# Message sums in four 128x32 tiles, edge products of a whole group in one burst, nodes two turns sooner

## The chip, the cores and the metric

One core of a Trainium2 chip runs the whole layer. The metric is the device time of one execution in microseconds (us); the time of the kernel before is the median of three runs.

## The reference, cut to what matters

One graph layer on 8192 nodes of 256 features and 131072 edges of 64 features, all float32. The edges come sorted by their destination `dst`.

```python
ea  = edge_attr @ w_e + b_e                       # 131072 x 256
msg = relu(x[src] + ea)
agg = segment_sum(msg, dst, num_segments=8192)
h_local = bn(relu((x + agg) @ w1 + b1) @ w2 + b2 + x)
# attention in 256 blocks of 32 nodes, 4 heads of 64
h_attn  = bn(softmax(q @ k.T / 8) @ v @ out_w.T + out_b + x)
out = h_local + h_attn
out = bn(out + relu(out @ m_w1 + m_b1) @ m_w2 + m_b2)
result = layernorm(x + out)
```

## The kernel before, in words

**Groups.** The edges are cut into 128 groups of 1024, a group into 8 tiles of 128 edges, two tiles to a "pair" q (512 pairs in all, four to a group). One group falls on some 64 neighbouring nodes.

**One pair's way.** GpSimd (POOL) gathers the rows x[src] of its two tiles with two indirect DMAs (line 368) into one of 8 buffers `xg`; it may overwrite the buffer when VectorE (DVE) has used it. DVE adds the bias and writes the sum into one of four banks `EA` of PSUM (`seed`, line 592). For that it waits for the gather and for the message of the pair four before (`s_msg`), which has the same bank. TensorE (PE) adds the edge products onto the bank (`products`, line 774; one call does two pairs with 4 matmuls of 64 rows, two side by side, in 8 instructions since a float32 matmul is two). ScalarE (ACT) takes the relu to `msg` (`message`, line 393).

**One group's sum.** DVE makes a one-hot matrix per tile (`make_onehot`, line 601): which of the W nodes of a window an edge belongs to. The group's tiles are split into SUB = 2 halves of TS = 4 tiles, each with its own window of W = 64 nodes that starts at the half's least `dst`. `sum_group` (line 789) multiplies one-hot and messages into bank `G`, half 0 to partitions 0 to 63 and half 1 to 64 to 127: 8 matmuls, 16 instructions. ACT copies `G` to `agg` (line 398), PE transposes it back into `G` (`transpose_agg`, line 798), and DVE adds the windows onto the columns of `aggT` (`add_agg`, line 624). The windows' places are data: `add_agg` begins with one `value_load` per window (line 608), which DVE's sequencer does, and only then waits and adds. Windows may overlap, so each add waits for the one before it. `sum_group(n)` waits with `s_added` until the windows of group n-1 are added, since both use `G`.

**Attention and nodes.** 16 slabs J of 512 nodes pass q, k, scores (`sc`), `soft`max, v and `av`; 22 blocks b of nodes pass w1, B (the products with out_w and w2), m1, m2, T (transposes) and the norm (`log`, `y`). 12 blocks have 512 nodes, 6 have 256, the last 4 have 128. PE works into one bank for attention and one for nodes, and each stage waits for the engine that empties the bank.

**Order.** Every engine runs its own list, in order, over 264 turns. The tables `HEADS`, `NODES`, `FIRST_256`, `NODES_128` and `SUMS` say in which turn a stage comes. Within a turn PE does products, the transposes of an earlier sum, a group's sum, attention, nodes; ACT does messages, copy, attention, nodes; DVE does seeds, `add_agg`, one-hot, attention, nodes. The queue of SP issues the loads of edge features (`load_ea`), xT, x rows (`xn`) and the stores, also turn by turn. Two turns make one group. In the steady part 16 turns (8 groups) serve one slab and one block.

**What is where before.** `products(t)` comes in every turn t, `seed(2t+2)` and `seed(2t+3)` in turn t, `sum_group(n)` in turn 2n+3 (2n+2 for the last four), its transposes and adds one turn later. Stage w1 of block b < 12 comes in turn 16b+21 and waits for the adds of all groups that reach its nodes and one more, and for the residual rows (line 688, in stage T) of the block before.

Of the kernel before, what the change touches and what calls it, by code (L numbers as in the profile page):

```python
# [31 lines left out]
BN_SCALE = 1.0 / (1.0 + 1e-5) ** 0.5  # L32
LN_EPS = 1e-5
PER = N // NG
SUB = 2
TS = TG // SUB
W = P // SUB
FULL = 512
NJ = N // FULL
RB = FULL // P  # L40
# [13 lines left out]
def heads_base(J):  # L54
# [7 lines left out]
         "T": (14, 15), "log": (15, 16), "y": (16, 17), "xn": (8, 9), "out": (17, 18)}  # L62
NODES_256 = {"w1": (0,), "B": (1,), "z": (2,), "m1": (2, 3), "m2": (4,), "T": (5,), "log": (6,),
             "y": (7,), "xn": (2,), "out": (8,)}
FIRST_256 = {12: 213, 13: 219, 14: 225, 15: 231, 16: 237, 17: 245}
NODES_128 = {
# [8 lines left out]
}  # L75
LASTB = 21


SUMS = {(2 * n + 3 if n < NG - 4 else 2 * n + 2): n for n in range(NG)}
TURNS = 264  # L80
CHUNKS = {"w1": CC, "B": CC, "m1": 2 * CC, "m2": CC}

# [20 lines left out]
def nodes_in(turn, stages):  # L103
    found = []
    for b in range(len(BLOCKS)):
        if b < 12:
            plan, base = NODES, 16 * b + 21
        elif b < 18:
            plan, base = NODES_256, FIRST_256[b]
        else:  # L110
            plan, base = NODES_128[b], 0
        found += [(b, s, n) for s in stages for n, at in enumerate(plan[s]) if base + at == turn]
    return found
# [25 lines left out]
def gnn_layer(nc, t, out):  # L139

    k = Kept()
    k.t, k.out = t, out
    k.sum_dram = nc.dram_tensor("sum_dram", (N, C), fp32, kind="Internal").ap()
    k.oT_dram = nc.dram_tensor("oT_dram", (IT, P, CC, NB), fp32, kind="Internal").ap()
    with ExitStack() as ctx:
        def sb(name, shape, dt=fp32):
            return ctx.enter_context(nc.sbuf_tensor(name, shape, dt))

        k.bank = [ctx.enter_context(nc.psum_tensor(f"bank{n}", [P, 512], fp32)) for n in range(8)]
        k.EA, k.G = k.bank[0:4], k.bank[4]  # L150
# [12 lines left out]
        k.bad = sb("bad", [P, 1])  # L163
        k.srcs = sb("srcs", [P, NG * TG], i32)
        k.rel = sb("rel", [P, NG, TG])
        k.we = sb("we", [P, C])
        k.iwT, k.owT = sb("iwT", [P, CC, 3 * C]), sb("owT", [P, CC, C])
        k.w1, k.w2 = sb("w1", [P, CC, C]), sb("w2", [P, CC, C])
        k.m1, k.m2 = sb("m1", [P, CC, 2 * C]), sb("m2", [P, 4, C])

        k.xg = sb("xg", [P, NX, 2 * C])
        k.ea = sb("ea", [P, NEA, 4 * P])
        k.msg = sb("msg", [P, NM, 2 * C])
        k.onehot = sb("onehot", [P, 2, TG, W])
        k.agg = sb("agg", [P, C])
        k.be_rows = k.agg

        k.xT = sb("xT", [P, NXT, CC, FULL])
        k.qT = sb("qT", [P, CC, FULL])
        k.kbd = sb("kbd", [P, CC, FULL // W, 2, W])  # L180
        k.vn = k.qT[:, :, :].rearrange("p c (a n) -> p (c a) n", n=C)
        k.dif, k.probT = sb("dif", [P, RB, H, NPG]), sb("probT", [P, 2, 2 * H, P])
        k.ex = k.prob = k.dif
        k.mx, k.sm, k.rs = sb("mx", [P, 2 * H]), sb("sm", [P, 2 * H]), sb("rs", [P, 2 * H])
        k.oT = sb("oT", [P, NOT, CC, FULL])

        k.h1, k.o = sb("h1", [P, CC, FULL]), sb("o", [P, CC, FULL])
        k.z, k.h2 = sb("z", [P, CC, FULL]), sb("h2", [P, 4, FULL])
        k.xn = sb("xn", [P, 2, 2, C])
        k.y = k.xn  # L190

        k.dst_g = k.h2[:, 0:2, :].rearrange("p c n -> p (c n)").bitcast(i32)
        k.dst_p = k.oT[:, 0, :, :].rearrange("p c (g t) -> p (c g) t", t=TG).bitcast(i32)
        k.gammas = k.xn[:, :, :, :].rearrange("p a b c -> p (a b) c")[:, 0:3, :]
        k.stats, k.mv = sb("stats", [P, 2, 2, 6]), sb("mv", [P, 2, 2, 2])
        k.logv, k.root = sb("logv", [P, 2, 2]), sb("root", [P, 2, 2])
        k.rstd, k.fix = sb("rstd", [P, 2]), sb("fix", [P, 2])
        program(nc, k)


def program(nc, k):
# [3 lines left out]
    with ExitStack() as ctx:  # L205
        def sem(name):
            return ctx.enter_context(nc.semaphore(name))
# [15 lines left out]
        s_seed, s_prod, s_msg = (sem(n) for n in ("s_x_seeded", "s_ea_product", "s_msg_made"))  # L223
        s_seg, s_agg, s_aggT, s_added = (sem(n) for n in (
            "s_group_summed", "s_agg_copied", "s_agg_transposed", "s_agg_added"))
        s_oh, s_half = sem("s_onehot_made"), sem("s_first_half_added")
        s_pre = [sem(f"s_agg_preloaded_{n}") for n in range(2)]

        s_xT = [sem(f"s_xT_loaded_{n}") for n in range(NXT)]
# [148 lines left out]
        def _(act):  # L378
# [21 lines left out]
            def attention(J, stage, n):  # L400
# [7 lines left out]
                if stage == "k":  # L408
# [3 lines left out]
                    for h in range(2):  # L412
                        of = slice(h * DH, (h + 1) * DH)
                        ins = nc.scalar.activation(
                            k.kbd[of, n, :, h, :], X[of, :].rearrange("p (r n) -> p r n", n=W),
                            ACT.Identity, bias=vecT[of, V_INB + 2 + n:V_INB + 3 + n])
                    ins.then_inc(s_qkc, 1)
                if stage == "soft":
# [45 lines left out]
                                         scale=-0.5).then_inc(s_root, 1)  # L464

            for turn in range(TURNS):
                for q in (2 * turn, 2 * turn + 1):
                    if q < NP:
                        message(q)
                if turn in SUMS:  # L470
                    copy_agg(SUMS[turn])
# [9 lines left out]
        def _(dve):  # L481
# [43 lines left out]
            for sub in range(SUB):  # L525
# [5 lines left out]
            step_of(ins)  # L531
            nc.vector.tensor_copy(k.base_i[:, :, :].rearrange("p s n -> p (s n)"),
                                  X[:, 0:SUB * P])
            step_of(nc.vector.tensor_reduce(k.bad[:, :], X[:, SUB * P:(SUB + 1) * P], AX.X,
                                            ALU.max))
            settle()
            nc.vector.tensor_copy(k.bad_i[:, :], k.bad[:, :]).then_inc(s_spread, 1)

# [68 lines left out]
            def add_agg(n):  # L607
# [11 lines left out]
                sums = G[:, 0:C].rearrange("p (c n) -> p c n", n=P)  # L619
                for sub in range(SUB):  # L620
                    if sub:
                        dve.wait_ge(s_half, n + 1)
                    window = aggT[:, :, bass.ds(at[sub], W)]
                    nc.vector.tensor_tensor(window, sums[:, :, sub * W:(sub + 1) * W], window,  # L624
                                            ALU.add).then_inc(s_added if sub else s_half, 1)

            def attention(J, stage, n):
                quarter = [slice(m * NPG, (m + 1) * NPG) for m in range(P // NPG)]
                scores = k.XA[:, :].rearrange("p (a n) -> p a n", n=W)
                dif = k.dif[:, 2 * n:2 * n + 2, :, :].rearrange("p r h n -> p (r h) n")  # L630
                if stage == "sc":
                    dve.wait_ge(s_sc, 2 * J + n + 1)
# [80 lines left out]
                                                      k.rstd[:, m:m + 1], ALU.subtract, ALU.mult)  # L713
                    ins.then_inc(s_y, 1)

            seed(0)
            seed(1)
            make_onehot(0)
            for turn in range(TURNS):
                for q in (2 * turn + 2, 2 * turn + 3):  # L720
                    if q < NP:
                        seed(q)
                if turn == 0:
                    nc.vector.memset(k.kbd[0:DH, :, :, 1, :], 0.0)
                    nc.vector.memset(k.kbd[DH:P, :, :, 0, :], 0.0).then_inc(s_kbd, 1)
                if turn == 1:
                    step_of(nc.vector.memset(k.probT[:, :, :, :], 0.0))
                    settle()
                if turn - 1 in SUMS:
                    add_agg(SUMS[turn - 1])  # L730
                if turn % 2 == 1 and 1 <= turn // 2 < NG:
                    make_onehot(turn // 2)
                weights(turn)
                for J, stage, n in heads_in(turn, ("sc", "soft")):
                    attention(J, stage, n)
# [7 lines left out]
        def _(pe):  # L743
# [12 lines left out]
                                           start=n == 0, stop=n == 3, skip_group_check=True)  # L756
            ins.then_inc(s_set, 1)
            pe.wait_ge(s_base, 1)
            for n, row in enumerate((k.lohi[:, 2, 0:1], k.lohi[:, 2, 1:2], k.lohi[:, 0, 0:1])):
                ins = nc.tensor.transpose(X[:, n * P:(n + 1) * P], row.to_broadcast([P, P]),  # L760
                                          ident[:, :])
            ins.then_inc(s_baseT, 1)
            pe.wait_ge(s_we, 16)

# [56 lines left out]
            def attention(J, stage, n):  # L821
# [13 lines left out]
                if stage == "sc":  # L835
# [4 lines left out]
                    for r in range(2):  # L840
                        for c in range(CC):
                            for m in range(2):
                                two = 4 * n + 2 * r + m
                                col = r * C + c * P
                                ins = nc.tensor.matmul(  # L845
                                    XA[m * W:(m + 1) * W, col:col + P],
                                    k.qT[:, c, two * W:(two + 1) * W],
                                    k.kbd[:, c, two, :, :].rearrange("p h n -> p (h n)"),
                                    start=True, stop=True)
                    ins.then_inc(s_sc, 1)  # L850
# [96 lines left out]
                    ins.then_inc(s_t, 1)  # L947

            for turn in range(TURNS):
                if turn < ND:  # L950
                    products(turn)
                if turn - 1 in SUMS:
                    transpose_agg(SUMS[turn - 1])
                if turn in SUMS:
# [315 lines left out]
```

## Time and profile before

| | |
|---|---|
| median of 3 runs | 1321.83 us (1321.43 to 1322.18) |
| profiled execution | 1321.81 us, its span 1321.8 us |
| PE busy | 1242.6 us (94%) |
| DVE, ACT, POOL busy | 819.9, 552.5, 970.7 us |
| granted TensorE clock | 0.98 of full speed on average |

Busy time is the union of an engine's instructions. Matmuls overlap, so PE's stretches are best read from one start to the next. DVE's sequencer reads window places beside its engine's work, and such time is not counted as busy. POOL's busy time leaves out 0.3 us between two gathers.

### The profile page before, as it was taken

To read this page: it belongs to the slowest core of one execution; us is meant where nothing else is said; L and a number is where in the kernel's file an instruction comes from. 1 tells how busy PE (TensorE), PEld (TensorE's weight loads), DVE (VectorE), ACT (ScalarE), POOL (GpSimd) and SP (SyncE) were. 2 spreads that over 40 slices of the span, in tenths; PEclk is the share of its full clock that TensorE was granted. 3 is DMA by queue.
4 is the path that set the end of the run, shared out by engine and by line. 5 is a ranking of instruction groups with operands and counts; after the bars stand their busy time and mean duration, and the time that the engine had idled before them with its cause. 6 is when DMAs were issued, how large, how long until landed. Compare 5 with 4: busy or idle time off the path is not lost.

```text
span 1321.8 us, 21000 instructions
## 1 busy us (share of the span) xinstructions
PE 1242.6 (94%) x7307; PEld 729.6 (55%) x7307; DVE 819.9 (62%) x1831; ACT 552.5 (42%) x1077; POOL 970.7 (73%) x1032
## 2 busy tenths in 40 slices
PE   5797999999999999999999999999999999999997
PEld 3454555555555555555555545555455556767676
DVE  4757456657475575746667475575746657548554
ACT  1343434444344434444443444443444434444443
POOL 7777777777777777777777777777777777777760
PEclk7897999999999999999999999999999999999999
DMA  9454645555555555555555555555555555545540
GB/s 325 137 177 144 180 136 160 170 173 177 158 155 168 170 169 162 177 160 162 170 162 177 152 156 167 170 170 155 162 176 164 168 158 155 184 146 151 178 140 18
DMA packets 113259, 216.02 MB, mean 163 GB/s; under 512 B 21505, under 2 KB 62721, under 8 KB 113153
## 3 DMA queue, kind: packets, MB, share of 16 engines
q0 software_dynamic: 49152, 134.28, 35.1%
q1 hardware_dynamic: 62560, 77.09, 18.1%
q10 hardware_dynamic: 1440, 3.29, 0.7%
q8 instruction: 59, 0.97, 0.3%
q14 instruction: 48, 0.39, 0.1%
HBM read 197.80 MB, written 16.78 MB: 162 GB/s over the span
## 4 chain that ended last, share of the span: by engine, by line
PE 55%; POOL 19%; DVE 11%; issue 9%; DMA 4%; DVEq 1%; ACT 1%
PE bank L746 28%; POOL xg L368 19%; PE bank L774 12%; PE bank L789 11%; DMA xg<-in_x_dram,srcs 4%; DVE bank L592 3%; PE bank L798 2%; DVE mx L635 2%; DVE dif L640 1%; PE bank L871 1%; PE bank L845 1%; DVEq L608 1%; DVE o L667 1%; DVE aggT L624 1%; DVE probT L656 1%
## 5 line engine op out<-in xcount | busy, mean ns | idle before, releaser
L368 POOL DMA_INDIRECT xg<-in_x_dram,srcs x1024 | 969.8, 947 | 313.5 <-issue 297.0
L393 ACT ACTIVATE msg<-bank 128x512 f32<-128x512 f32 x512 | 277.7, 594 | 392.7 <-PE bank L774 392.2
L592 DVE TENSOR_TENSOR bank<-xg,bank 128x512 f32<-128x512 f32 x512 | 337.3, 690 | 157.8 <-DMA xg<-in_x_dram,srcs 132.4
L774 PE MATMUL bank<-we,ea 64*128 64x256 f32 x2048 | 297.8, 410 | 55.5 <-DVE bank L592 55.5
L774 PEld LDWEIGHTS bank<-we,ea 64*128 64x128 f32 x2048 | 182.0, 190 | 205.4 <-issue 146.8
L789 PE MATMUL bank<-msg,onehot 128*64 128x256 f32 x2048 | 254.7, 392 | 4.0 <-DVE aggT L624 4.0
L789 PEld LDWEIGHTS bank<-msg,onehot 128*64 128x64 f32 x2048 | 139.8, 139 | 103.7 <-issue 47.8
L624 DVE TENSOR_TENSOR aggT<-bank,aggT 128x128 f32 x256 | 74.7, 292 | 187.4 <-PE bank L798 142.7
L746 PE MATMUL bank<-xT,iwT 128*128 128x512 f32 x256 | 125.8, 614 | 6.6 <-DMA xT<-in_xT_dram 6.6
L746 PE MATMUL bank<-o,m 128*128 128x512 f32 (+2 forms) x352 | 122.8, 483 | 0.0
L746 PE MATMUL bank<-h,m 128*128 128x512 f32 (+2 forms) x352 | 116.8, 479 | 1.0 <-ACT h L453 1.0
L398 ACT COPY agg<-bank 128x256 f32<-128x256 f32 x128 | 47.6, 372 | 113.1 <-PE bank L789 113.1
L601 DVE TENSOR_TENSOR onehot<-bank,rel 128x512 f32<-128x512 f32 x128 | 87.6, 684 | 0.2
L746 PEld LDWEIGHTS bank<-h,m 128*128 128x128 f32 x352 | 60.1, 191 | 40.4 <-issue 36.9
L746 PEld LDWEIGHTS bank<-o,m 128*128 128x128 f32 x352 | 59.6, 191 | 31.2 <-issue 28.2
L676 DVE TENSOR_TENSOR z<-bank,z 128x512 f32<-128x512 f32 (+2 forms) x44 | 23.1, 543 | 86.3 <-PE bank L746 86.1
L453 ACT ACTIVATE h<-bank,mb 128x512 f32<-128x512 f32 (+2 forms) x88 | 47.6, 569 | 68.2 <-PE bank L746 68.2
L746 PEld LDWEIGHTS bank<-xT,iwT 128*128 128x128 f32 x256 | 44.1, 192 | 51.4 <-issue 51.0
L746 PE MATMUL bank<-oT,owT 128*128 128x512 f32 (+2 forms) x176 | 64.6, 491 | 0.6 <-ACT h L439 0.6
L746 PE MATMUL bank<-iwT,xT 128*128 128x256 f32 x256 | 64.3, 396 | 0.0
L746 PE MATMUL bank<-h,w 128*128 128x512 f32 (+2 forms) x176 | 62.2, 477 | 0.0
L746 PE MATMUL bank<-aggT,w 128*128 128x512 f32 (+2 forms) x176 | 61.3, 480 | 0.8 <-DVE xn L688 0.8
(88 smaller groups left out, 927.0 us busy)
## 6 DMA issues: line engine op xcount, KB each, us to landing
ea<-in_ea_dram SPq DMA_DIRECT2D x128, 256.0 KB
xg<-in_x_dram,srcs POOLq DMA_INDIRECT x1024
xT<-in_xT_dram SPq DMA_DIRECT2D x32, 256.0 KB, 3.9
aggT<-in_xT_dram SPq DMA_DIRECT2D x32, 256.0 KB, 5.0
oT_dram<-oT SPq DMA_DIRECT2D x32, 256.0 KB
xn<-in_x_dram SPq DMA_DIRECT2D x32, 256.0 KB, 5.1
out_dram<-xn SPq DMA_DIRECT2D x30, 256.0 KB, 2.8
m<-in_m_dram ACTq DMA_DIRECT2D x2, 512.0 KB, 17.9
```

The costliest lines, as they stand in the source:

```text
L368: pool.indirect_dma_start(xg[:, q % NX, n * C:(n + 1) * C], None, t["x"], bass.IndirectOffsetOnAxis(k.srcs[:, at:at + 1], 0)).then_inc(s_x ...
L393: nc.scalar.activation(msg[:, q % NM, :], EA[q % 4][:, :], ACT.Relu).then_inc(s_msg, 1)
L398: nc.scalar.copy(k.agg[:, :], G[:, 0:C]).then_inc(s_agg, 1)
L453: ins = nc.scalar.activation(k.h2[:, c, at], bank(b, "m1")[:, of], ACT.Relu, bias=k.mb1[:, c:c + 1])
L592: nc.vector.tensor_tensor(EA[q % 4][:, :].rearrange("p (a c) -> p a c", a=2), xg[:, q % NX, :].rearrange("p (a c) -> p a c", a=2), KB[:, 0 ...
L601: nc.vector.tensor_tensor(onehot[:, n % 2, :, :], KB[:, C:C + W].unsqueeze(1).to_broadcast([P, TG, W]), k.rel[:, n, :].unsqueeze(2).to_bro ...
L624: nc.vector.tensor_tensor(window, sums[:, :, sub * W:(sub + 1) * W], window, ALU.add).then_inc(s_added if sub else s_half, 1)
L635: ins = nc.vector.tensor_reduce(k.mx[g, :], scores[g, :, own], AX.X, ALU.max)
L746: ins = nc.tensor.matmul(to, stationary(c), moving(c), start=start and c == 0, stop=stop and c == blocks - 1, skip_group_check=skip)
L774: ins = nc.tensor.matmul(EA[(2 * d + pair) % 4][:, two * C:(two + 1) * C], ea[rows, n % NEA, at:at + P], k.we[rows, :], start=False, stop= ...
L789: ins = nc.tensor.matmul(G[sub * W:(sub + 1) * W, 0:C], onehot[:, n % 2, at, :], msg[:, q % NM, two * C:(two + 1) * C], start=tile == 0, s ...
L798: ins = nc.tensor.transpose(G[:, c * P:(c + 1) * P], k.agg[:, c * P:(c + 1) * P], ident[:, :])
```

## The change

SUB becomes 4: four sub-groups of two tiles, each with a window of 32 nodes and 32 partitions of `G`; the sum still takes 8 matmuls, of 32 instead of 64 columns of the one-hot. `add_agg` reads four places and makes four adds, each after the one before. The one-hot has 256 instead of 512 elements in a partition. Products of a whole group (two calls) come in turn 2n, its sum in turn 2n+1, transposes and adds in turn 2n+2. The seeds of group n+1 come in turn 2n: two, then the adds of group n-1, then two. The one-hot of group n+1 comes in turn 2n+1. All stages of nodes come two turns sooner (the last block one). Attention stays in its turns; it had used W = 64 for its own layout and now uses GW = 64.

```diff
-SUB = 2
+SUB = 4
 TS = TG // SUB
 W = P // SUB
+GW = 2 * NPG
-FIRST_256 = {12: 213, 13: 219, 14: 225, 15: 231, 16: 237, 17: 245}
+FIRST_256 = {12: 211, 13: 217, 14: 223, 15: 229, 16: 235, 17: 243}
...
-SUMS = {(2 * n + 3 if n < NG - 4 else 2 * n + 2): n for n in range(NG)}
+SUMS = {2 * n + 1: n for n in range(NG)}
...
-            plan, base = NODES, 16 * b + 21
+            plan, base = NODES, 16 * b + 19
...
 # ScalarE, each turn
-                for q in (2 * turn, 2 * turn + 1):
-                    if q < NP:
+                if turn % 2 == 0 and turn // 2 < NG:
+                    for q in range(2 * turn, 2 * turn + PG):
                         message(q)
...
 # add_agg
                 for sub in range(SUB):
                     if sub:
-                        dve.wait_ge(s_half, n + 1)
+                        dve.wait_ge(s_part, (SUB - 1) * n + sub)
                     window = aggT[:, :, bass.ds(at[sub], W)]
                     nc.vector.tensor_tensor(window, sums[:, :, sub * W:(sub + 1) * W], window,
-                                            ALU.add).then_inc(s_added if sub else s_half, 1)
+                                            ALU.add
+                                            ).then_inc(s_added if sub == SUB - 1 else s_part, 1)
...
 # VectorE, each turn
-                for q in (2 * turn + 2, 2 * turn + 3):
-                    if q < NP:
-                        seed(q)
+                ahead = turn // 2 + 1
+                if turn % 2 == 0 and ahead < NG:
+                    seed(PG * ahead)
+                    seed(PG * ahead + 1)
+                if turn - 1 in SUMS:
+                    add_agg(SUMS[turn - 1])
+                if turn % 2 == 0 and ahead < NG:
+                    seed(PG * ahead + 2)
+                    seed(PG * ahead + 3)
...
-                if turn - 1 in SUMS:
-                    add_agg(SUMS[turn - 1])
-                if turn % 2 == 1 and 1 <= turn // 2 < NG:
-                    make_onehot(turn // 2)
+                if turn % 2 == 1 and ahead < NG:
+                    make_onehot(ahead)
...
 # TensorE: setup spreads four window starts instead of two (and the check value into G)
-            for n, row in enumerate((k.lohi[:, 2, 0:1], k.lohi[:, 2, 1:2], k.lohi[:, 0, 0:1])):
+            for n, row in enumerate(k.lohi[:, 2, sub:sub + 1] for sub in range(SUB)):
...
 # TensorE, each turn
-                if turn < ND:
+                if turn % 2 == 0 and turn < ND:
                     products(turn)
+                    products(turn + 1)
```

## Rows read from the trace of the kernel before

**Rows 1.** The page's chain that ended last, shares of the span by engine.

```profile
PE 55%; POOL 19%; DVE 11%; issue 9%; DMA 4%; DVEq 1%; ACT 1%
```

**Rows 2.** Line 368, the gathers: duration ns min/median/max, first and last start.

```profile
L368 POOL DMA_INDIRECT xg<-in_x_dram,srcs x1024: 940/946/1397, 3.4 to 1284.1; - x171
```

**Rows 3.** Waits, whole span: who waited for whom, us in total, times, longest.

```profile
POOL xg L368 <- DVE bank L592: 14.8, 48, 0.4
...
PE bank L789 <- DVE aggT L624: 4.0, 7, 1.0
```

**Rows 4.** Timeline of PE: start, us, line, out<-in, count [idle before <-releaser].

```profile
425.74 1.14 PE L774 MATMUL bank<-we,ea 64*128 64x256 f32 x8
426.80 1.95 PE L789 MATMUL bank<-msg,onehot 128*64 128x256 f32 x16
428.58 1.04 PE L871 MATMUL bank<-probT,qT 128*64 128x128 f32 x16
429.55 1.13 PE L774 MATMUL bank<-we,ea 64*128 64x256 f32 x8
430.62 0.44 PE L798 MATMUL bank<-ident,agg 128*128 128x128 f32 x2
430.89 3.60 PE L746 MATMUL bank<-h,m 128*128 128x512 f32 x8
...
446.30 1.88 PE L746 MATMUL bank<-aggT,w 128*128 128x512 f32 x4
```

**Rows 5.** Timeline of PE, the one regular wait, in two periods of 16 turns.

```profile
400.52 1.14 PE L774 MATMUL bank<-we,ea 64*128 64x256 f32 x8 [2.39 <-DVE bank L592]
...
478.46 2.04 PE L774 MATMUL bank<-we,ea 64*128 64x256 f32 x8 [2.39 <-DVE bank L592]
```

**Rows 6.** Stretch after the second: us, busy by engine, granted clock, DMA.

```profile
480.00:482.00 2.00, 2.00 (x9) 1.39 (x6) 1.93 (x5) 1.08 (x2) 1.39 (x3) 0.51 1.12 391
```

**Rows 7.** Timeline early: products, their messages, a seed that waits for these.

```profile
30.60 1.14 PE L774 MATMUL bank<-we,ea 64*128 64x256 f32 x8
...
31.78 1.09 ACT L393 ACTIVATE msg<-bank 128x512 f32<-128x512 f32 x2 [0.39 <-PE bank L774]
...
32.48 1.29 DVE L592 TENSOR_TENSOR bank<-xg,bank 128x512 f32<-128x512 f32 x2 [1.65 <-ACT msg L393]
```

**Rows 8.** Line 608, the reads of window places, by DVE's sequencer.

```profile
L608 DVEq TENSOR_LOAD <-base_i x256: 297/305/954, 36.4 to 1302.0; - x128
```

**Rows 9.** Timeline of DVE: a seed, and the adds after two reads.

```profile
616.28 0.70 DVE L592 TENSOR_TENSOR bank<-xg,bank 128x512 f32<-128x512 f32 x1 [0.96 <-DMA xg<-in_x_dram,srcs]
617.72 0.72 DVE L624 TENSOR_TENSOR aggT<-bank,aggT 128x128 f32 x2 [0.74 <-issue]
```

**Rows 10.** Groups by line and shape: busy us, mean ns | idle before.

```profile
L624 DVE TENSOR_TENSOR aggT<-bank,aggT 128x128 f32 x256 | 74.7, 292 | 187.4 <-PE bank L798 142.7 <-issue 25.6 <-DVE aggT L624 1.0
...
L499 DVE COPY bank<-iota 128x64 f32<-128x64 f32 x1 | 0.2, 228 | 1.8 <-POOL even L357 1.8
```

**Rows 11.** Timeline of DVE: scores (two lines) and softmax, up to the next seeds.

```profile
698.98 1.71 DVE L635 TENSOR_REDUCE mx<-bank 32x8 f32<-32x256 f32 x4
700.72 1.72 DVE L640 TENSOR_TENSOR dif<-bank,mx 32x256 f32<-32x256 f32 x4
...
704.94 0.41 DVE L647 TENSOR_REDUCE sm<-dif 128x8 f32<-128x256 f32 x1
...
707.90 1.29 DVE L592 TENSOR_TENSOR bank<-xg,bank 128x512 f32<-128x512 f32 x2
```

**Rows 12.** Timeline of PE: products of turns 46 and 254, the last sum.

```profile
256.12 1.13 PE L774 MATMUL bank<-we,ea 64*128 64x256 f32 x8
...
1289.90 1.14 PE L774 MATMUL bank<-we,ea 64*128 64x256 f32 x8
...
1298.11 1.95 PE L789 MATMUL bank<-msg,onehot 128*64 128x256 f32 x16
```

**Rows 13.** Chain of waits, in order of time: a gather, from issue to landing.

```profile
731.06 2.74 DMA xg<-in_x_dram,srcs
```

More of the change, by code:

```diff
@@ L179, in gnn_layer @@
         k.qT = sb("qT", [P, CC, FULL])
-        k.kbd = sb("kbd", [P, CC, FULL // W, 2, W])
+        k.kbd = sb("kbd", [P, CC, FULL // GW, 2, GW])
         k.vn = k.qT[:, :, :].rearrange("p c (a n) -> p (c a) n", n=C)
@@ L225, in program @@
             "s_group_summed", "s_agg_copied", "s_agg_transposed", "s_agg_added"))
-        s_oh, s_half = sem("s_onehot_made"), sem("s_first_half_added")
+        s_oh, s_part = sem("s_onehot_made"), sem("s_window_added")
         s_pre = [sem(f"s_agg_preloaded_{n}") for n in range(2)]
@@ L414, in attention @@
                         ins = nc.scalar.activation(
-                            k.kbd[of, n, :, h, :], X[of, :].rearrange("p (r n) -> p r n", n=W),
+                            k.kbd[of, n, :, h, :], X[of, :].rearrange("p (r n) -> p r n", n=GW),
                             ACT.Identity, bias=vecT[of, V_INB + 2 + n:V_INB + 3 + n])
@@ L533, in _ @@
                                   X[:, 0:SUB * P])
-            step_of(nc.vector.tensor_reduce(k.bad[:, :], X[:, SUB * P:(SUB + 1) * P], AX.X,
-                                            ALU.max))
+            step_of(nc.vector.tensor_reduce(k.bad[:, :], G[:, 0:P], AX.X, ALU.max))
             settle()
@@ L621, in add_agg @@
                     if sub:
-                        dve.wait_ge(s_half, n + 1)
+                        dve.wait_ge(s_part, (SUB - 1) * n + sub)
                     window = aggT[:, :, bass.ds(at[sub], W)]
                     nc.vector.tensor_tensor(window, sums[:, :, sub * W:(sub + 1) * W], window,
-                                            ALU.add).then_inc(s_added if sub else s_half, 1)
+                                            ALU.add
+                                            ).then_inc(s_added if sub == SUB - 1 else s_part, 1)
             def attention(J, stage, n):
                 quarter = [slice(m * NPG, (m + 1) * NPG) for m in range(P // NPG)]
-                scores = k.XA[:, :].rearrange("p (a n) -> p a n", n=W)
+                scores = k.XA[:, :].rearrange("p (a n) -> p a n", n=GW)
                 dif = k.dif[:, 2 * n:2 * n + 2, :, :].rearrange("p r h n -> p (r h) n")
@@ L714, in node @@
                     ins.then_inc(s_y, 1)
-            seed(0)
-            seed(1)
+            for q in range(PG):
+                seed(q)
             make_onehot(0)
             for turn in range(TURNS):
-                for q in (2 * turn + 2, 2 * turn + 3):
-                    if q < NP:
-                        seed(q)
+                ahead = turn // 2 + 1
[7 more added lines that the diff above has]
+                    seed(PG * ahead + 3)
                 if turn == 0:
@@ L758, in _ @@
             pe.wait_ge(s_base, 1)
-            for n, row in enumerate((k.lohi[:, 2, 0:1], k.lohi[:, 2, 1:2], k.lohi[:, 0, 0:1])):
+            for n, row in enumerate(k.lohi[:, 2, sub:sub + 1] for sub in range(SUB)):
                 ins = nc.tensor.transpose(X[:, n * P:(n + 1) * P], row.to_broadcast([P, P]),
                                           ident[:, :])
+            ins = nc.tensor.transpose(G[:, 0:P], k.lohi[:, 0, 0:1].to_broadcast([P, P]),
+                                      ident[:, :])
             ins.then_inc(s_baseT, 1)
@@ L845, in attention @@
                                 ins = nc.tensor.matmul(
-                                    XA[m * W:(m + 1) * W, col:col + P],
-                                    k.qT[:, c, two * W:(two + 1) * W],
+                                    XA[m * GW:(m + 1) * GW, col:col + P],
+                                    k.qT[:, c, two * GW:(two + 1) * GW],
                                     k.kbd[:, c, two, :, :].rearrange("p h n -> p (h n)"),
```

16 rows, old and new, of the table NODES_128 are left out of this document.

## The prediction

> **What bounds the kernel now.** I read the chain first, then the waits, then the timelines. The chain gives PE 55% and POOL 19% [rows 1], so two engines compete. The gathers are a metronome: 1024 starts from 3.4 to 1284.1 us [rows 2], one per 1.252 us, and what POOL waited for buffers is 0.3 us each time [rows 3], no more than its gap between any two gathers. Eight groups (64 gathers) so cost 80.1 us whatever else is done, and the kernel ends 37 us after the last gather. PE is nearly as full: in its timeline each burst starts where the one before stops [rows 4], and its one regular wait of 2.39 us returns after 478.46 - 400.52 = 77.9 us, which is 16 turns or 8 groups [rows 5]. With that pace it catches up with the gathers by 2 us per 8 groups. Sums never really wait for the adds: 4.0 us in all [rows 3]. A change thus gains only in the 37 us at the end, but loses as soon as some loop needs over 10.0 us per group.
>
> **The change, part by part.** Times of PE are from start to start [rows 4]: products 1.06, transposes 0.27, sum 1.78, av 0.97, m2 or B 3.6, w1, q, k, v or one use of m1 1.8. Scores I take like av.
>
> *Sum.* Still 16 instructions. No row shows 32 columns; below, four side by side need half the time of two, 0.9 us; above, no gain, 1.78 (side by side not at all: 3.6). I take 0.95, since 64 columns show what side by side does. PE gains 0.85 per group, and two products in one burst 1.9 instead of 2.1: about 1.05 in all, 8.4 per 8 groups. Alone this moves nothing, as the gathers don't get faster.
>
> *Adds.* Two reads of window places become four, two adds four. From a seed's start to the add behind it pass 617.72 - 616.28 = 1.44 us with two reads [rows 9], though the data were there ("issue"); a read begins with a load of 0.305 [rows 8] and takes 0.6 with its checks. Four: 2.65 us. An add of 128 columns takes 0.292 and starts 0.43 after the one before (0.72 for two [rows 9, 10]); with 64 columns I take 0.225 like the copy of that size [rows 10], bounds 0.15 and 0.29, so 0.36 apart and 1.3 for four. The one-hot halves, 0.3 us less on DVE.
>
> *Order.* This decides. Before, a turn's seeds wait for messages of the turn before, so DVE can run ahead and reads the places early. Now the first seeds of group n+1 wait for messages of group n, whose products come in the same turn; the reads stand behind these seeds, the adds of n-1 behind the reads, and the sum of n, one turn later, behind the adds. From the start of a burst: message 1.18 later, seed 0.70 after that [rows 7], sum 1.88; second seed issued 0.45 later; reads 2.65; adds 1.3; a semaphore 0.1. So a sum starts at least 6.4 us after its burst, where PE has only 1.9 + 0.27 + the even turn's attention and nodes (E) to do. Then 0.95 for the sum and the odd turn's work (O). A pair of turns takes the larger of 7.35 + O and 3.1 + E + O. Queued behind the sum are O and the next products; behind the adds on DVE two seeds, the scores, softmax and residual adds.
>
> *Steady part.* With the new tables, by turn modulo 16:
> - 14, 15: E m2, O av: 8.4.
> - 0, 1: m2; av, T. T waits for the z add behind the seeds, 8.45: 9.05.
> - 2, 3: T; w1. w1 waits for the residual rows of T, behind four seeds on DVE (7.7 + 0.7): 10.25, though PE works 5.5.
> - 4, 5: q, w1; q: 9.2.
> - 6, 7: k, B; k: 10.35.
> - 8 to 13: DVE bound. Scores 3.45, softmax 2.95 [rows 11]. The first burst is late by k's and z's copies on ACT: seeds and adds end at 8.8; scores, o 0.75, one-hot 0.35, softmax: 16.3; seeds, adds, seeds (reads hidden) 4.05, scores, one-hot, softmax: 27.1; seeds and adds: sum of turn 13 at 29.9; with v and m1 34.5.
>
> Sum 81.75 per 8 groups, against 77.9 that PE and DVE need before and 80.1 of the gathers: the new loop is slower than both.
>
> *Last part.* Turns 210 to 253, 22 pairs in which blocks come denser (256 nodes per 6 turns). By the same rule: 10.25, 12.2, 12.75, then 28.0 for turns 216 to 219 (w1 behind the residual rows behind the scores, then m1 behind y, scores and o on DVE), 12.75, 10.25, 10.5, 10.95, 11.05, 12.2, 25.4 for turns 232 to 235 likewise, 12.2, 11.9, 8.4, 9.2, 10.5, 11.95, 9.3, 10.6, 9.3: 249.7.
>
> *End.* From the products of turn 254 to the last sum 7.4 (w1 of block 20 now waits for adds of the same turn). From the last sum to the end: 1321.8 - 1298.1 = 23.7 before [rows 12]; block 20 is one turn further ahead and the sum shorter, 2 less, while four reads and adds cost 1.7 and the norm of block 20 stands ahead of block 21's rows, 1.2: 24.65.
>
> *The rest.* Nodes two turns sooner keep their distance from the sums, so nothing by itself; their loads and stores pass SP's queue in front of loads of edge features, 0.3 to 0.6 us each, two turns ahead of need: 0, and if that cover went, a load late by as much per block, below 20 us. Setup: one transpose more, four subtractions for two, a larger cast, 0.9 us ahead of seeds that wait for their first gathers: 0, at worst 0.9. POOL's waits: four buffers free in one burst, needed two groups later; with the loop late, POOL waits for it.
>
> **The sum.** Turn 46 starts at 256.1 before [rows 12]. Up to there the start's costs are alike (first gathers, loads of weights), so I keep it, within -4 and +8. Ten times 81.75 to turn 206, 17.45 to turn 210, 249.7 to turn 254, 7.4 and 24.65: 256.1 + 817.5 + 17.45 + 249.7 + 7.4 + 24.65 = 1372.8, say **1372 us**, 50 slower (3.8%). The profiled execution (1321.81) and the median (1321.83) agree, so nothing is added. An error of 0.2 us in the 6.4 makes some 15 us over 128 groups. If the middle stays below 80.1, the gathers set it, and turn 210 starts with the first four tiles of group 105: 3.4 + 105 x 10.015 + 3 x 1.252 + 2.74 + 0.7 = 1062 [rows 2, 13], which ends at 1344. Own range 1340 to 1402.
>
> *The clock.* After the wait of 2.39 us the products took 2.04 instead of 1.14 [rows 5], and the granted clock was 0.51 in 480 to 482, the lower level [rows 6]; after 400.52 it stayed high. So such a wait can cost 1.7 us of PE. The new order makes waits of 3.7 (turn 2) and 4.0 (turn 10) in each 16 turns, before work on the loop: 0 to 2 x 1.7 per 8 groups, up to 30 us. I take none, but the upper end reaches there. The Trainium skill (TensorE: Matmul & The Clock Gate, "HAM oscillation") says that idle gaps in a loop throttle the clock again, and speaks against the change; by it the sum would be about 1400.
>
> **Rivals.**
> - *The loop stays below the gathers, so the change is faster.* For it: PE's work falls to 67 of 80 us. It decides if the sum starts less than about 5.5 us after its burst, so if reads overlap the seeds or messages come sooner. Then the last data land at 1284.1 + 2.74 = 1286.85 [rows 2, 13]; seed 0.7, products 1.15, messages 1.1: 1289.8; with PE's work in between the last sum starts at 1290.4, not 1298.1, and the end is 1315. Against: rows 9, where reads cost time with a seed running.
> - *It cancels*: the middle on the gathers, and in the last part lag only as large as before: 1319 to 1324.
> - *32-column tiles don't run four at a time*, so that the change doesn't do what it says: sums 0.85 longer in nearly every pair, 6 per 8 groups and 19 at the end, so about 1450. Against: two at a time do so now.
>
> **Chances.** Forecast 0.72, of which the gathers bound the middle in about a third; faster 0.14; cancelled 0.07; no four-fold tiles 0.07. Range 1322 to 1402: it leaves out the faster case and what lies above. What a measurement can tell from no change is 0.2%, 2.6 us: faster 0.14, same 0.07, slower 0.79.
>
> **What would show it.** Right: PE waits before line 789 grow from 4 us to some 2 us per group, with DVE's adds as releaser; the sum's 16 instructions take about 1 us; adds start 2.6 us after the second seed; gathers wait for seeds in the second half, or the time from the last gather to the end grows far beyond 37 us. Wrong: PE's waits stand before line 774 with the gathers behind them, gathers keep 1.252 us, and the end comes within 32 us of the last.

## The result, and the profile after

The changed kernel takes 1462.4 us (median of 4 runs, 1455.8 to 1462.7) against 1322.0 of the kernel before: ratio 1.105, 95% interval 1.1037 to 1.1064. The forecast was 1372 us with a range of 1322 to 1402: the direction was right, the size was not; the loss is 140 us, where 50 were forecast.

The page's chain of the changed kernel, by engine and then by line. Beside [rows 1] POOL has left it, and DVE's sequencer (DVEq) has grown from 1% to 15%, nearly all of it the reads of window places (L608).

```profile
PE 42%; DVE 25%; DVEq 15%; issue 10%; ACT 7%; DMA 1%; SPq 0%
PE bank L751 23%; DVEq L608 13%; PE bank L796 8%; PE bank L781 7%; DVE aggT L624 7%; DVE bank L592 6%; ACT msg L394 4%; DVE dif L641 3%; DVE mx L636 3%; PE bank L878 2%; DVEq L624 1%; DVE probT L657 1%; ACT z L448 1%; ACT kbd L415 1%; DMA xT<-in_xT_dram 1%
```

Its waits, as us in total, times, longest. The sums (L796) waited 4.0 us for the adds [rows 3], now 198.8; the gathers waited 14.8 us for the seeds, now 145.1. The second row shown is DVE standing ahead of its adds for what the profile calls issue: the reads.

```profile
DVE bank L592 <- ACT msg L394: 284.5, 86, 6.8
DVE aggT L624 <- issue: 208.4, 119, 2.4
...
PE bank L796 <- DVE aggT L624: 198.8, 106, 6.5
POOL xg L369 <- DVE bank L592: 145.1, 74, 8.3
```

One regular pair of turns (142, 143) in PE's timeline. Products come as one burst, and the sum has the short form (16 instructions of 32 columns take 1.07 us, those of 64 columns 1.95 before; from its start to the next instruction 1.00 and 1.78 [rows 4]), but it starts 6.48 us after the burst's start, with PE waiting for the last 0.68:

```profile
794.51 2.00 PE L781 MATMUL bank<-we,ea 64*128 64x256 f32 x16
796.44 0.44 PE L805 MATMUL bank<-ident,agg 128*128 128x128 f32 x2
796.72 3.60 PE L751 MATMUL bank<-h,m 128*128 128x512 f32 x8
800.99 1.07 PE L796 MATMUL bank<-msg,onehot 128*32 128x256 f32 x16 [0.68 <-DVE aggT L624]
```

The same loop on DVE in these turns: two seeds at +1.88, 1.86 us of issue (the first of the 2.4 us of reads run beside the second seed), four adds from +5.03, and only then the other two seeds.

```profile
796.39 1.29 DVE L592 TENSOR_TENSOR bank<-xg,bank 128x512 f32<-128x512 f32 x2 [5.14 <-ACT msg L394]
799.54 1.30 DVE L624 TENSOR_TENSOR aggT<-bank,aggT 128x64 f32 x4 [1.86 <-issue]
800.76 1.28 DVE L592 TENSOR_TENSOR bank<-xg,bank 128x512 f32<-128x512 f32 x2
```

The instructions of line 608: duration ns min/median/max, first and last start. A read is a load and, to check its bounds, a register operation and an assertion; with the gaps that makes 0.61 us, and the four stand one after the other.

```profile
L608 DVEq TENSOR_LOAD <-base_i x512: 296/304/668, 31.4 to 1441.4; - x171
L608 DVEq FUSED_REGOPS  x512: 183/183/206, 32.0 to 1441.7; - x171
L608 DVEq SEQ_ASSERT  x512: 23/23/35, 32.2 to 1442.3; - x171
```

Twice per 16 turns the wait is longer, and there the clock falls. PE's timeline at turn 66 and, below it, the window behind (columns: length of the window, busy time and count of PE, PEld, DVE, ACT, POOL, granted clock, DMA share, GB/s):

```profile
473.50 0.60 PE L952 MATMUL bank<-ident,z 128*128 128x128 f32 x4
477.82 1.93 PE L796 MATMUL bank<-msg,onehot 128*32 128x256 f32 x16 [3.73 <-DVE aggT L624]
479.69 3.55 PE L751 MATMUL bank<-aggT,w 128*128 128x512 f32 x4
```

```profile
478.00:483.00 5.00, 5.00 (x20) 1.65 (x15) 3.90 (x13) 0.87 (x3) 3.78 (x5) 0.51 0.37 107
```

Behind the wait of 3.73 us the granted clock is 0.51, the lower level of 1.2 GHz; the sum takes 1.93 instead of 1.07 and w1 3.55 instead of 1.88. Over the whole span the granted clock stands below full for 267 us, before for 64.

By the starts of the products in PE's timeline, in the profiled executions (the spans are 1321.8 and 1461.0):

| stretch | before | forecast | after |
|---|---|---|---|
| start to turn 46 | 256.1 | 256.1 | 282.1 |
| turns 46 to 205, per 8 groups | 79.0 | 81.75 | 85.5 |
| turns 206 to 209 | 17.6 | 17.45 | 18.0 |
| turns 210 to 253 | 225.9 | 249.7 | 276.2 |
| turn 254 to the end | 31.9 | 32.05 | 29.9 |

### The profile page after: what moved, and what is told of

Same layout as the page of the kernel before. It is cut to its first block, busy times and chain, and to the rows that moved or that the text cites. A ratio compares the mean times of both kernels' runs of the same rounds, so it can differ in the third digit from the quotient of the medians.

```text
span 1461.0 us, 22286 instructions
## 1 busy us (share of the span) xinstructions
PE 1195.7 (82%) x7309; PEld 692.5 (47%) x7309; DVE 821.4 (56%) x2089; ACT 541.6 (37%) x1077; POOL 970.4 (66%) x1032
## 3 DMA queue, kind: packets, MB, share of 16 engines
q0 software_dynamic: 49152, 134.28, 31.9%
## 4 chain that ended last, share of the span: by engine, by line
PE 42%; DVE 25%; DVEq 15%; issue 10%; ACT 7%; DMA 1%; SPq 0%
PE bank L751 23%; DVEq L608 13%; PE bank L796 8%; PE bank L781 7%; DVE aggT L624 7%; DVE bank L592 6%; ACT msg L394 4%; DVE dif L641 3%; DVE mx L636 3%; PE bank L878 2%; DVEq L624 1%; DVE probT L657 1%; ACT z L448 1%; ACT kbd L415 1%; DMA xT<-in_xT_dram 1%
## 5 line engine op out<-in xcount | busy, mean ns | idle before, releaser
L796 PE MATMUL bank<-msg,onehot 128*32 128x256 f32 x2048 | 160.4, 436 | 198.8 <-DVE aggT L624 198.8
L394 ACT ACTIVATE msg<-bank 128x512 f32<-128x512 f32 x512 | 264.4, 602 | 99.1 <-PE bank L781 97.5
L781 PE MATMUL bank<-we,ea 64*128 64x256 f32 x2048 | 266.5, 401 | 6.5 <-DVE bank L592 6.5
L624 DVE TENSOR_TENSOR aggT<-bank,aggT 128x64 f32 x512 | 115.1, 225 | 264.3 <-issue 208.4
L781 PEld LDWEIGHTS bank<-we,ea 64*128 64x128 f32 x2048 | 194.6, 194 | 106.2 <-issue 83.2
L796 PEld LDWEIGHTS bank<-msg,onehot 128*32 128x32 f32 x2048 | 67.1, 119 | 302.8 <-issue 289.2
L751 PE MATMUL bank<-o,m 128*128 128x512 f32 (+2 forms) x352 | 144.1, 550 | 10.2 <-DVE o L668 10.2
L751 PE MATMUL bank<-aggT,w 128*128 128x512 f32 (+2 forms) x176 | 88.2, 650 | 15.7 <-DVE xn L689 10.4
L751 PEld LDWEIGHTS bank<-aggT,w 128*128 128x128 f32 x176 | 40.7, 256 | 53.2 <-issue 28.5
L415 ACT ACTIVATE kbd<-bank,vecT 64x512 f32<-64x512 f32 x64 | 43.7, 682 | 41.3 <-PE bank L751 40.9
## 6 DMA issues: line engine op xcount, KB each, us to landing
m<-in_m_dram ACTq DMA_DIRECT2D x2, 512.0 KB, 15.5
```

Of the source, the lines that this page charges most:

```text
L394: nc.scalar.activation(msg[:, q % NM, :], EA[q % 4][:, :], ACT.Relu).then_inc(s_msg, 1)
L415: ins = nc.scalar.activation(k.kbd[of, n, :, h, :], X[of, :].rearrange("p (r n) -> p r n", n=GW), ACT.Identity, bias=vecT[of, V_INB + 2 + ...
L751: ins = nc.tensor.matmul(to, stationary(c), moving(c), start=start and c == 0, stop=stop and c == blocks - 1, skip_group_check=skip)
L781: ins = nc.tensor.matmul(EA[(2 * d + pair) % 4][:, two * C:(two + 1) * C], ea[rows, n % NEA, at:at + P], k.we[rows, :], start=False, stop= ...
L796: ins = nc.tensor.matmul(G[sub * W:(sub + 1) * W, 0:C], onehot[:, n % 2, at, :], msg[:, q % NM, two * C:(two + 1) * C], start=tile == 0, s ...
```

## The experiments

The theory: the sum-adds loop rules each pair, and the reads in it are the price. Rivals: the new dependence itself costs, with or without reads; the four-fold tiles cost; the falling clock costs.

**The reads moved out of the loop** (`e1_reads_early`), issued at the end of DVE's odd turn.

```diff
-            def add_agg(n):
-                at = [nc.vector.value_load(k.base_i[0:1, sub, n:n + 1], min_val=0, max_val=N - W)
-                      for sub in range(SUB)]
+            def places(n):
+                return [nc.vector.value_load(k.base_i[0:1, sub, n:n + 1], min_val=0, max_val=N - W)
+                        for sub in range(SUB)]
+            def add_agg(n, at):
...
# end of each turn of VectorE
+                if turn in SUMS:
+                    at = places(SUMS[turn])
```

> The changed kernel with one edit: the four window places are read at the end of the odd turn, not between the seeds and the adds; everything else as changed. Loop theory (the four reads stand between a group's seeds and the sum that waits): the sum starts 4.6 us after its burst instead of 6.5, the two regular waits of 3.7 us in 16 turns shrink to about 1.9, the clock falls less often, and 8 groups take about 80.1 us (the gathers) instead of 85.5; time 1325 to 1360. Rival, the order itself (seeds and adds behind messages of the same turn): reads are hidden anyway and the time stays within 1% of 1462. Rival, the 32-column sums: no change.

1373.2 us, ratio 1.0377 (1.0359 to 1.0394): 89 us back, but short of what was expected. In DVE's timeline the adds now follow the seeds at once:

```profile
675.06 1.29 DVE L592 TENSOR_TENSOR bank<-xg,bank 128x512 f32<-128x512 f32 x2 [5.14 <-ACT msg L394]
676.26 1.29 DVE L626 TENSOR_TENSOR aggT<-bank,aggT 128x64 f32 x4
```

Where DVE has much to do the four reads stand between its last work and the next seeds, which do not need them. In turns 2 and 12 of 16 these then start some 4.5 and 3.5 to 4.4 us after the burst, where the changed kernel has 1.88 and mostly 2.4; in turn 10 DVE is late in both (6.9 here, 7.4 there). A read moved is still a read. Turn 130, whose burst is at 689.28:

```profile
693.75 1.29 DVE L592 TENSOR_TENSOR bank<-xg,bank 128x512 f32<-128x512 f32 x2 [2.60 <-issue]
```

**The adds ahead of all four seeds** (`e2_adds_first`).

```diff
                 if turn % 2 == 0 and ahead < NG:
-                    seed(PG * ahead)
-                    seed(PG * ahead + 1)
                 if turn - 1 in SUMS:
                     add_agg(SUMS[turn - 1])
                 if turn % 2 == 0 and ahead < NG:
-                    seed(PG * ahead + 2)
-                    seed(PG * ahead + 3)
+                    for q in range(PG * ahead, PG * ahead + PG):
+                        seed(q)
```

> The changed kernel with one edit: in even turns the reads and adds of the group before come ahead of all four seeds. Loop theory: the adds then wait only for the transposes (2.3 us after the burst's start) and end 3.8 us after it, so the sum no longer waits where the even turn has 1.5 us of work; 8 groups at the pace of the gathers; time 1318 to 1350. Seeds start 3.7 instead of 1.9 us after the burst, which by the order theory (messages and seeds are what is late) would make it slower than 1462.

1364.0 us, ratio 1.0308 (1.0291 to 1.0326), above what was expected again. The loop through the seeds is cut, but the reads remain in DVE's queue, and in turns 2, 10 and 12 of 16 the adds start 4.6, 6.5 and 4.3 to 7.4 us after the burst instead of the 2.5 of most others. How much of the remaining loss is the reads' was not taken apart.

**The order without the tiles** (`e3_order_only`), and **the tiles without the order** (`e4_tiles_only`).

```diff
# e3, on the changed kernel
-SUB = 4
+SUB = 2
# e4, on the kernel before (windows, waits and setup of the change follow from it)
-SUB = 2
+SUB = 4
```

> The new order alone, with two sub-groups of 64 nodes as before: two reads, two adds, sums of 1.8 us. Loop theory: the sum starts about 1.9 + 0.45 + 1.45 + 0.7 + 0.1 = 4.6 us after its burst, 1.9 sooner than changed, but is 0.85 longer, so pairs of turns need 6.4 + O instead of 7.4 + O: 1360 to 1400. Rival, 32-column sums are at fault: 1315 to 1322, as before. Rival, the order without regard to reads and adds: 1440 to 1480.

> The four tiles of 32 columns alone (four reads, four adds, shorter sums) in the order of before. Loop theory: reads are done ahead there, PE gains 0.85 us per group, the gathers stay at 1.252 us each: 1312 to 1322. Rival, reads and adds cost DVE time wherever they stand: 1340 or more. Rival, 32-column sums are at fault: over 1400.

e3: 1353.5 us, 1.0236 (1.0208 to 1.0264), just below its band. e4: 1323.9 us, 1.0009 (0.9999 to 1.0018): not the gain that was expected, but no loss either, with the same four reads and four adds. In the old order the sum of pair 142 starts 14.1 us after the pair's first products and the adds that it needs end at 11.1: 3 us of reserve cover the reads. (In turn 2 of 16 there is no such reserve, and the sum waits 1.2 to 2.4 us.) What PE saves in e4 it waits elsewhere: 86.5 us for the seeds, 55.5 before.

```profile
PE bank L777 <- DVE bank L592: 86.5, 41, 5.8
PE bank L792 <- DVE aggT L624: 28.4, 19, 2.4
```

The two halves cost some 31 and 1 us, together 140. What only the whole change has is the new order together with four reads, or with the short tiles; e6 and e7 below tell these apart.

**The clock held** (`e5_clock_held`): PE filled with matmuls whose result is not used, where it waits longest.

```diff
+            def fill(to):
+                for _ in range(7):
+                    nc.tensor.matmul(to[:, 0:C], ident[:, :], k.we[:, :], start=True, stop=True)
...
# m1, first use
                         pe.wait_ge(s_o, before(b + 1, "B"))
+                        if b < 12:
+                            fill(to)
...
# end of each turn of TensorE
+                if turn % 16 == 2 and 50 <= turn <= 206:
+                    pe.wait_ge(s_oc, ...)
+                    fill(k.XA)
```

> The changed kernel, with seven more matmuls of 128x256 (some 3 us, their result is not used) on PE twice per 16 turns: at the end of turn 2 of the 16, and ahead of the first m1 in turn 10, where PE otherwise waits 3.7 to 3.8 us for the adds. Theory A (these waits lower the clock, and the work right behind them, which is on the loop, pays for it): the sums of turns 3 and 11 take 1.07 instead of 1.93 us, the first pair falls from 12.0 to 10.3 us, the two pairs 10 and 12 together from 26.9 to about 24.5, 4 us per 16 turns, 10 times: about 1462 - 40 = 1420 us (1410 to 1430), and the time at the lower clock falls from 266 to below 100 us. Theory B (the lower clock stands only where PE would wait anyway): no gain, 1455 to 1470.

1436.6 us, 1.0876 (1.0857 to 1.0896): 26 us back, less than expected. In the pair at turn 2 of 16 it does what was said (12.0 to 10.14 us); PE's timeline at turn 130:

```profile
714.96 3.19 PE L758 MATMUL bank<-we,ident 128*128 128x256 f32 x14
718.85 1.07 PE L800 MATMUL bank<-msg,onehot 128*32 128x256 f32 x16 [0.70 <-DVE aggT L624]
720.55 1.98 PE L751 MATMUL bank<-aggT,w 128*128 128x512 f32 x4 [0.63 <-DVE xn L689]
```

The pairs at turns 10 and 12 go only from 26.9 to 25.6 (one round, 15.80 + 11.13 and 13.21 + 12.38): pair 10 gains 2.6, and pair 12 gives half of it back. The middle falls from 85.5 to 82.8 per 8 groups, start and last part stay (280.3, 276.9), and the time below full clock falls from 267 to 142 us. So 27 us of the loss are undone by holding the clock in the middle, where it falls because of the waits.

**No reads** (`e6_no_reads`): the true places are left out, the rest is the changed kernel.

```diff
-                at = [nc.vector.value_load(k.base_i[0:1, sub, n:n + 1], min_val=0, max_val=N - W)
-                      for sub in range(SUB)]
+                at = [min(64 * n + 16 * sub, N - W) for sub in range(SUB)]
```

> The changed kernel with the windows' places written out as constants (64n + 16 per window), so that the four reads of window places are gone; the true places depend on dst, so this part of the computation is left out. Theory A (the four reads in the loop are the main cost): the sum starts 4.0 to 4.6 us after its burst instead of 6.48, pairs at turn 14 and 0 fall back to PE's own work of about 7.5, and the whole to 1320 to 1350 us. Theory B (the dependence sum-adds-seeds itself is the cost, the reads overlap with it): above 1400 us. In between, 1350 to 1400: the reads are the larger part and the order costs the rest, as with 64-column tiles.

1330.2 us, 1.0059 (1.0042 to 1.0076): 132 of the 140 us are gone. PE's timeline of the pair at turn 126; the sum starts at +5.73 with no wait at all:

```profile
653.66 2.00 PE L780 MATMUL bank<-we,ea 64*128 64x256 f32 x16
655.59 0.44 PE L804 MATMUL bank<-ident,agg 128*128 128x128 f32 x2
655.86 3.60 PE L750 MATMUL bank<-h,m 128*128 128x512 f32 x8
659.39 1.07 PE L795 MATMUL bank<-msg,onehot 128*32 128x256 f32 x16
```

The same stretches as in the table above: 254.3, 79.9, 16.1, 231.5, 27.9. Start, middle and last part all come back, so the reads had cost in all of them. The clock still stands below full for 175 us, and with that only 8 us are left to explain: the clock by itself, without the waits for the adds, is not the main cause.

**The order with two places, each read twice** (`e7_order_reads_twice`): four reads beside the old tiles.

```diff
# on e3
+                for sub in range(SUB):
+                    nc.vector.value_load(k.base_i[0:1, sub, n:n + 1], min_val=0, max_val=N - W)
```

> The new order with 128x64 tiles (SUB = 2, 1353.5 us), with each of the two places read twice, so four reads as in the changed kernel, and the old tiles, sums of 1.95 us and two adds. Theory A (the number of reads ahead of the adds explains the difference between 1353 and 1462): sum at about +5.9 us instead of +4.7, some 0.8 to 1.2 us more in most of the 128 pairs, 1420 to 1460 us. Theory B (the shorter sums leave PE idle, the clock falls, and that explains the difference): 1355 to 1385 us.

1453.3 us, 1.1014 (1.0979 to 1.1049): two more reads whose values nobody uses turn 1353 into 1453. The granted clock stands below full for 136 us here, half of the 267 of the changed kernel, so a loss of this size does not need that much of the lower clock. DVE's timeline shows the same 1.85 us of issue, and PE's the sum at +5.90:

```profile
792.72 1.29 DVE L592 TENSOR_TENSOR bank<-xg,bank 128x512 f32<-128x512 f32 x2 [5.50 <-ACT msg L394]
795.87 0.72 DVE L626 TENSOR_TENSOR aggT<-bank,aggT 128x128 f32 x2 [1.85 <-issue]
```

```profile
790.84 2.00 PE L783 MATMUL bank<-we,ea 64*128 64x256 f32 x16
...
796.74 1.95 PE L798 MATMUL bank<-msg,onehot 128*64 128x256 f32 x16
```

**The reads shortened**, in two steps. `e9_reads_unchecked` drops the bounds at the read; `e12_reads_without_check` states them and leaves the check out altogether.

```diff
# e9
-                at = [nc.vector.value_load(k.base_i[0:1, sub, n:n + 1], min_val=0, max_val=N - W)
+                at = [nc.vector.value_load(k.base_i[0:1, sub, n:n + 1])
# e12
+                at = [nc.s_assert_within(
+                    nc.vector.value_load(k.base_i[0:1, sub, n:n + 1]), 0, N - W,
+                    skip_runtime_bounds_check_because="dst >= 0, and base is min(lo, N - W)")
```

> The changed kernel with its four reads of window places kept, but without their check against bounds: in the changed kernel's trace a read takes 0.61 us of DVE's sequencer, the load 0.30, the register operation of the check 0.18, the assertion 0.02 and gaps; without the check 0.33 is left, 1.3 instead of 2.4 us for four. Theory (the time of the reads in the loop is what costs, by its length): adds at +3.9, sum at +5.3 to +5.4 instead of +6.48 after its burst; between the kernel without reads (1330) and the changed one (1462), 1340 to 1395 us, nearer to the lower end because in many pairs PE's own work then ends last. Rival (what costs is that a register is needed at all, not how long reading it takes): 1430 to 1462.

e9: 1498.8 us, 1.1323 (1.1306 to 1.134), slower still and outside both bands. The check had not gone: it moved to the use, with one register operation and two assertions more at each add (line 624: duration ns min/median/max; one register operation per add is there with checked reads too), between the adds and so in the same loop.

```profile
L624 DVEq FUSED_REGOPS  x1024: 52/118/206, 35.4 to 1482.1; - x171
L624 DVEq SEQ_ASSERT  x1024: 23/23/35, 35.7 to 1482.2; - x171
```

The sum of turn 142 (its burst is at 815.80 here) stands at +6.71, 0.23 us later than in the changed kernel. In turn 10 of 16 it is 0.9 us later (11.2 instead of 10.3), since there the reads had been hidden beside DVE's other work, and the checks between the adds are not: the adds start 0.70 instead of 0.36 us apart. All 128 groups cost 36 us more:

```profile
822.51 1.07 PE L796 MATMUL bank<-msg,onehot 128*32 128x256 f32 x16 [0.91 <-DVE aggT L624]
```

> The changed kernel with its four reads of window places, but with no check against bounds, neither at the read nor at the use (without bounds given at the read, the check went to each add, 0.34 us four times, and the sum started at +6.71 instead of +6.48 and the time rose from 1462 to 1499). Only the four loads are left, 0.33 us each, 1.3 instead of 2.4 us per group. Theory (the length of the reads ahead of the adds is the cost): adds from +3.9, sum at about +5.35 where PE allows it (PE's own work ends at +5.73 in turns 14 and 0), 1330 to 1370 us, close to the kernel without reads (1330). Rival (a register read at run time costs by itself): 1400 us or more.

e12: 1356.6 us, 1.0267 (1.0245 to 1.0289), as the theory expected. Only the loads are left (its line 609); in turn 126 the adds end at +5.2 and the sum starts where PE is ready, at +5.73. The middle is back at 79.4 us per 8 groups; the start (262.8) and turns 210 to 253 (253.1) stay above the kernel without reads.

```profile
L609 DVEq TENSOR_LOAD <-base_i x512: 297/308/737, 33.2 to 1335.5; - x171
```

```profile
658.24 2.00 PE L783 MATMUL bank<-we,ea 64*128 64x256 f32 x16
...
663.97 1.07 PE L798 MATMUL bank<-msg,onehot 128*32 128x256 f32 x16
```

With the order fixed, then, 0, 1.3, 2.4 us of reads, and 2.7 of reads and checks, give 1330, 1357, 1462 and 1499 us: the length of what stands ahead of the sum decides, and steeply once the sum waits in most groups: for the adds it waits in 106 of 128 in the changed kernel, in 53 in e12.

**Looking for a version that beats both.** `e10_new_order_best` is e2 with two places and e9's reads; `e8_new_end_only` and `e11_last_two_sums` are the kernel before with only the sums of its last six or two groups one turn sooner.

```diff
# e10, on e2
-SUB = 4
+SUB = 2
-                at = [nc.vector.value_load(k.base_i[0:1, sub, n:n + 1], min_val=0, max_val=N - W)
+                at = [nc.vector.value_load(k.base_i[0:1, sub, n:n + 1])
# e8 (END = NG - 6; blocks 17 to 21 as changed, adds ahead of seeds for n >= END)
# and e11 (END = NG - 2; blocks 20 and 21 as changed)
+SUMS = {(2 * n + 3 if n < END - 4 else 2 * n + 2 if n < END else 2 * n + 1): n for n in range(NG)}   # e8
+SUMS = {(2 * n + 3 if n < NG - 4 else 2 * n + 2 if n < END else 2 * n + 1): n for n in range(NG)}    # e11
-                if turn % 2 == 1 and 1 <= turn // 2 < NG:
+                if turn % 2 == (turn // 2 < END) and 1 <= turn // 2 < NG:
```

> The new order with 128x64 tiles (two places), the adds ahead of all four seeds, and the reads without their check: 0.66 us of reads per group instead of 2.4. Theory (the new order is no worse than the old once the reads are short and ahead of nothing): the middle at the gathers' pace, turn 206 at 1052 to 1060, the time 1318 to 1335 us. Rival (the order itself costs, since messages, seeds and sums of a burst follow each other in one turn): 1336 to 1353 us.

> The kernel before, with its old order and 128x64 tiles up to group 121; only the last six groups have their sum in turn 2n+1, their adds ahead of the seeds and their one-hot a turn sooner, and the last five blocks have the turns of the changed kernel. Theory (the new order is worth its 2 us only behind the last gather, where nothing waits for gathers any more): turn 254 starts at 1287 to 1290 as before, the end comes 28.5 to 30 us later instead of 32, 1316 to 1320 us, ratio 0.996 to 0.999. Rival (the sums now wait for messages of the same turn and PE stands still in each of the last six groups): 1322 to 1330 us.

> The kernel before, only with the sums of the last two groups one turn sooner and blocks 20 and 21 two and one turns sooner, as in the changed kernel. Theory (the end behind the last gather is 2 us shorter with these tables, and in the last two groups no pair is hurt): turn 254 at 1289 to 1291, the end 29 to 30.5 us later, 1318 to 1321 us, ratio 0.997 to 0.9995. Rival (the sums wait for messages of their own turn, and the end only moves the wait): 1321 to 1327 us.

e10: 1349.4 us, 1.0209 (1.0195 to 1.0223). As in e9, its checks moved to the adds, which start 0.76 us apart (2.84 and 3.60 us after the burst of turn 142) instead of 0.43, so it does not test reads without checks; e2's order with the reads of e12 was not run. Its middle runs at the gathers' pace (79.6 per 8 groups, turn 206 at 1058.4, as expected), but the start takes 262.1 and turns 210 to 253 241.4, 15.5 more than before. e8: 1337.2 us, 1.0115 (1.0098 to 1.0131): the end behind turn 254 is 30.1 instead of 31.9, but turns 210 to 253 take 241.0. e11: 1326.5 us, 1.0031 (1.002 to 1.0042): its end takes 32.4, so it gains nothing there. e10 and e11 land where their rivals were put and e8 beyond both; what holds the last part back in them was not taken apart. No version here beats the kernel before.

## Why the prediction was wrong

**What was right.** The mechanism is the forecast's: sum behind adds, adds behind reads, reads behind seeds, seeds behind messages of the same turn. The sum was put at 6.4 us after its burst and stands at 6.48; first seed 1.88 and 1.88; adds from 5.03 (4.98 forecast), 1.30 long (1.3); the sum itself 1.00 from start to start (0.95). The end was put at 32.05 and took 29.9: the last sum came 5.3 instead of 7.4 us after its products. The waits of 3.7 and 3.8 us in turns 2 and 10 are where they were expected. The rivals fall: the tiles run four at a time, and with four checked reads in it the loop is slower than the gathers.

**Where it failed.** Three terms of the sum, together 90 us (the end gave 2 back):

- *The start*, 26 us. The step: "Up to there the start's costs are alike (first gathers, loads of weights), so I keep it, within -4 and +8." The loop holds there too: from turn 8 on, sums of the changed kernel start 6.5 us or more after their burst. Without reads turn 46 is at 254.3, with short ones at 262.8, with four checked ones at 282.1. The working applied its own rule to turns 46 to 253 and not to the 23 groups ahead of them.
- *The middle*, 37 us. The step: "I take none" for the clock. The middle takes 85.5 instead of 81.75 per 8 groups. With the clock held (e5) 8 of the 10 rounds of 16 turns take 82.2 to 82.6, near the forecast, and two in which it fell all the same 84.2 and 84.5. So about 3 us of each round are the clock, 27 in all in that run, near the upper end of 30 that the text had named and not taken; the other 0.7 per round is the rule's own error. The row [rows 5] had shown the price: products behind such a wait took 2.04 instead of 1.14. The Trainium skill (TensorE: Matmul & The Clock Gate, "HAM oscillation") says that idle gaps in a loop throttle the clock again each time round; the trace agrees, with 0.51 behind the wait of 3.73 us.
- *The last part*, 26.5 us. The step: "By the same rule: 10.25, 12.2, 12.75 ...: 249.7." The loop's pairs are near (11.3, 12.1, 12.8), but turns 216 to 219 took 32.5 instead of 28.0, and the pairs at 242, 246, 248 and 250 took 12.4, 13.5, 13.4 and 12.3 instead of 9.2, 11.95, 9.3 and 10.6; sums of 1.93 us in 242, 246 and 250 show the low clock there. Without reads the part takes 231.5. The mean granted clock of this part fell from 0.99 to 0.90, that of the start from 0.91 to 0.86; how much of either loss is the clock alone was not measured, since e5 filled only the middle.

Besides, "an error of 0.2 us in the 6.4 makes some 15 us" was too small: e9, whose sums start later by 0.23 us or somewhat more in most pairs and by 0.9 in turn 10 of 16, cost 36, of which 11 lie in the start and 10 in turns 210 to 253. In total the clock stood below full no longer than in the changed kernel (270 us against 267).

**Where the 140 us went.** 132 to four reads of 0.61 us in a loop without reserve (e6); 26 come back if the clock alone is held in the middle (e5), and these overlap with the 132. The rest, 8, is what the change costs without its reads (e6 against the kernel before).

## What to carry to other kernels

When a change puts a producer and its consumer into the same turn, write down the whole loop and its reserve; an instruction that cost nothing under 3 us of reserve (four reads in e4) can cost 1 us per group without it. Apply such a rule to the whole span, start and end included, and price the clock behind each new wait by the rows that show it. A place that is read at run time is work of the engine's sequencer in queue order: shorten or drop its checks before moving it.

## What the runs showed of the hardware

- A read of a window place takes 0.61 us of DVE's sequencer with its check and 0.33 to 0.34 without. Instructions behind it in DVE's queue started only when it was done, with the engine idle: the adds after 1.86 us of issue in turn 142, in e1 even seeds that need no place, after 2.60. A check left out at the read came back at each use, 0.34 us each (e9).
- Sixteen instructions of 128x32 columns, four tiles side by side, take 1.07 us, of 128x64 1.95.
- Matmuls whose result nobody uses held the clock: behind 3.19 us of them the sum took 1.07 instead of 1.93.
